# A transformer block on one core: the rows of the attention stacks reordered, and the first batch's loads and sends rearranged

## The chip, the cores and the metric

The kernel runs on one core of a Trainium2 chip. A core has TensorE (matrix products), VectorE (DVE), ScalarE (ACT), GpSimd (POOL), and SyncE (SP), which here only sends DMA transfers. The metric is the device time of one execution in microseconds; lower is better.

## The reference

Four batches of 512 tokens with 128 channels go through one pre-norm block, in float32:

```python
x = x + attn(layernorm(x))     # 16 heads of 8 channels, causal, position slopes on the keys
x = x + ffn(layernorm(x))      # 8 experts, all are summed, times a gate of the token

# attn
scores = q @ k.T / sqrt(8) + slope[head] * key_position      # -inf above the diagonal
y = softmax(scores) @ v ; return y @ w_proj + b_proj
# ffn
logits = rms_normalised(x @ gate_w.T + gate_b) * rms_w ; g = max(softmax(logits / 0.5))
h = gelu(einsum('nd,edh->neh', x, w1) + b1) ; y = einsum('neh,ehd->ned', h, w2) + b2
return (y * g / (g + 1e-6)).sum(axis=1)
```

## The kernel before

**Heads in stacks.** The 16 heads are worked on in 4 sets (s) of 4 heads (q). A head has only 8 channels, so one product serves all rows of the array: `q_stack[i]` holds, for each set, 128 rows by 512 tokens, and `k_stack` holds, for each set and head of it, 128 rows by 512 tokens. To keep float32 precision each value is split into a high and a low part, and a score is the sum of three terms: q_hi with k_hi, q_hi with k_lo, and q_lo with k_hi. Before the change the rows are ordered by term, head and channel: term g of the three fills rows 32 g to 32 g + 31. Rows 96 to 127 hold the position slopes (two rows a head) and, from row 104, the maximum of each query's scores as a high and a low row. The product over 128 rows then gives the finished score; rows of k_stack that belong to other heads are zero.

**How the stacks are filled.** Projection products write q and k of a batch to PSUM; VectorE adds the bias (`take_q`, `take_k`) into `q_full` and `k_full`, ScalarE makes the high parts (`split_high`), GpSimd the low ones (`split_low`). Then DMA transfers inside the core copy them into the stacks. `load_q` sends three transfers of 256 KB: source all 128 rows of q_hi or q_lo, destination 32 rows of the stack. `load_k` (high, SyncE) and `load_k_low` (low, GpSimd) send transfers of 32 KB, for one term, head and half (two sets), each with 8 rows as destination, through `send_k`. `load_max` sends the negated maxima of one set as two transfers of 8 KB. q_stack has two buffers, k_stack one, which is refilled by halves.

**A set's work.** For each set TensorE first computes the scores with zero maxima (`max_unit`, line 720) into the ring `v_ring`; VectorE takes each row's maximum (line 1047). The maxima are transposed, negated (`take_max`) and sent to the stack. Then TensorE computes the scores again, transposed, with the maxima in (`exp_unit`, line 742, and the causal mask, line 748), ScalarE takes the exponential (line 553), and `pv` (line 767) multiplies with v. Beside this, the later stages of the batch before (normalisation, gate, the feed-forward products of lines 673 to 675 and 835) are spread over the 16 places of each set.

**What sets the order.** Every engine runs its own list in program order and waits on semaphores. The places of each unit are written out in tables (`EARLY_PLAN`, `LATER_PLAN`, `STAGES`), which the change leaves alone. The first maximum unit of a batch waits for all three q transfers (`q_loaded`) and for the k transfers of its head. Each DMA-sending engine sends its transfers in the order of its list; SyncE and ScalarE would use two hardware queues, but before the change ScalarE sends nothing.

**The first batch.** It has nothing ahead of it to hide behind. SyncE loads x, w_attn, the constants (580 KB: identity, causal mask, key constants, query constants), the biases and w1. GpSimd clears zeros, makes two small masks, clears rows 0 to 95 of k_stack in two halves (`k_zeros`), and splits w_attn. ScalarE writes the constant rows 96 to 127 of both stacks (`q_constants`, `k_constants`), then makes q_hi and k_hi. TensorE transposes the normalised x, projects q, k and v, and begins the maximum units.

Of the kernel before, what the change touches and what calls it, by code (L numbers as in the profile page):

```python
# [50 lines left out]
CONST_ROWS = 96  # L51
ALIBI_ROWS, MAX_ROWS = 96, 104
# [45 lines left out]
def block_kernel(nc, x, w_attn, w_proj, w1, w2, columns, rows, consts, out):  # L98
# [20 lines left out]
    with ExitStack() as ctx:  # L119
# [103 lines left out]
        cst_loaded = sem("cst_loaded")  # L223
        wa_loaded = sem("wa_loaded")
# [17 lines left out]
        k_zeros = sem("k_zeros")  # L242
# [104 lines left out]
        def _(sp):  # L347
# [10 lines left out]
            def load_q(b):  # L358

                if b >= 2:  # L360
                    sp.wait_ge(e_filled, UNITS * SETS * (b - 1))
                    sp.dma_start(q_stack[b % 2][MAX_ROWS:MAX_ROWS + 2 * QUADS, :, :].bitcast(F32),
                                 zeros[0:2 * QUADS * SETS, :]).then_inc(q_loaded, 16)
                for g, part in ((0, 0), (1, 0), (2, 1)):
                    sp.wait_ge(q_split, 2 * b + part + 1)
                    sp.dma_start(q_stack[b % 2][QR * g:QR * (g + 1), :, :].bitcast(F32),
                                 (q_hi, q_lo)[part][:].bitcast(F32)).then_inc(q_loaded, 16)

            def load_k(b, half):


                if b == 0:
                    sp.wait_ge(k_zeros, half + 1)
                else:

                    sp.wait_ge(e_filled, UNITS * (SETS * (b - 1) + 2 * half + 2))
                sp.wait_ge(k_split, 2 * b + 1)
                for q in range(QUADS):
                    for g in (0, 2):
                        send_k(sp, k_hi, half, g, q, k_loaded[half][q])  # L380

            def load_max(b, s):
                sp.wait_ge(m_ready, SETS * b + s + 1)
                for r, part in ((MAX_ROWS, m_hi), (MAX_ROWS + QUADS, m_lo)):
                    sp.dma_start(q_stack[b % 2][r:r + QUADS, s, :].bitcast(F32),
                                 part[:].bitcast(F32)).then_inc(m_loaded, 16)
# [39 lines left out]
        def _(pool):  # L426
# [22 lines left out]
            def load_k_low(b, half):  # L449

                if b == 0:
                    pool.wait_ge(k_zeros, half + 1)
# [34 lines left out]
            pool.wait_ge(zeros_set, 1)  # L487
            pool.affine_select(out=ident_bf[:], in_=zeros[:, 0:P], compare_op=ALU.not_equal, fill=1.0, base=0,
# [3 lines left out]
            pool.memset(k_stack[0:CONST_ROWS, 0:2, :, :].bitcast(F32), 0.0).then_inc(k_zeros, 1)  # L492
            pool.wait_ge(wa_loaded, 16)
            split(w_attn_sb[:], w_attn_hi[:], w_attn_lo[:], wa_split, 0)
            settle(pool.memset(v_ones[0][:], 0.0))
# [42 lines left out]
        def _(act):  # L538
# [57 lines left out]
            def q_constants(i):  # L596
                for s in range(SETS):
                    act.activation(q_stack[i][CONST_ROWS:P, s, :], zeros[CONST_ROWS:P, :], ACT.Identity,
                                   bias=cst[CONST_ROWS:P, C_QUERY + s:C_QUERY + s + 1]).then_inc(q_const, 1)

            def k_constants(half):
                for q in range(QUADS):
                    act.activation(k_stack[CONST_ROWS:P, 2 * half:2 * half + 2, q, :],  # L603
                                   cst[CONST_ROWS:P, C_KEY:C_KEY + T].unsqueeze(1).to_broadcast([QR, 2, T]),
                                   ACT.Copy, scale=cst[CONST_ROWS:P, C_QUAD + q:C_QUAD + q + 1]).then_inc(k_const, 1)
# [44 lines left out]
        def _(pe):  # L650
# [27 lines left out]
            def transpose_x(b):  # L678
                pe.wait_ge(xn_ready, b + 1)
                if b == 0:  # L680
                    pe.wait_ge(cst_loaded, 16)
# [196 lines left out]
            transpose_x(0)  # L878
            project_qk(0, 0)
            project_qk(0, 1)  # L880
# [52 lines left out]
        def _(dve):  # L933
# [80 lines left out]

            def take_k(b):
                bank_ = v_bank()
                if b >= 1:
# [166 lines left out]
            take_xT(0)  # L1184
            take_q(0)
            take_k(0)
            take_v(0)
            dve.wait_ge(cst_loaded, 16)
# [28 lines left out]
def constants(H, T):  # L1217

    import numpy as np

    SETS = H // QUADS
    c = np.zeros((P, C_QUAD + QUADS), np.float32)
    c[:, C_IDENT:C_IDENT + P] = np.eye(P)
    c[:, C_MASK + T - P:C_MASK + T] = np.where(np.arange(P)[None, :] > np.arange(P)[:, None], MASKED, 0.0)
    slopes = (2.0 ** (-(8.0 / H) * np.arange(1, H + 1))).astype(np.float32)
    high = (slopes.view(np.uint32) & np.uint32(0xFFFFF000)).view(np.float32)
    c[ALIBI_ROWS:MAX_ROWS, C_KEY:C_KEY + T] = np.arange(T)
    c[MAX_ROWS:MAX_ROWS + 2 * QUADS, C_KEY:C_KEY + T] = 1.0
    for q in range(QUADS):
        heads = slice(QUADS * q, QUADS * q + SETS)  # L1230
        c[ALIBI_ROWS + q, C_QUERY:C_QUERY + SETS] = high[heads]
        c[ALIBI_ROWS + QUADS + q, C_QUERY:C_QUERY + SETS] = (slopes - high)[heads]
        c[CONST_ROWS + q:P:QUADS, C_QUAD + q] = 1.0
    return c


def qk_order(a):
# [5 lines left out]
    q = q.reshape(-1, QUADS, 4, 8).swapaxes(-1, -2)  # L1243
# [34 lines left out]
```

## Time and profile before

| what | us |
|---|---|
| median of 3 runs (lowest, highest) | 338.78 (338.53, 339.36) |
| profiled execution, its own time | 340.44 |
| span of its profile | 338.6 |
| TensorE products busy | 298.2 (88%) |
| ScalarE busy | 194.1 (57%) |
| VectorE busy | 190.0 (56%) |
| GpSimd busy | 84.5 (25%) |
| hardware DMA queue | 11.90 MB, 16.2% of 16 engines |

The span is counted from the profile's first instruction. Times at the start of a row are microseconds from there. "SPq" marks SyncE's sends; their time is that of sending, not of the transfer. Short names after an L are lines of the kernel above. Most of the busy time is TensorE's; the question is where it stands still, and for what. PEclk, the clock granted to TensorE, is given as a share of 2.4 GHz: 1.00 is 2.4 GHz and 0.50 is 1.2 GHz.

### The profile page before, as it was taken

To read this page: it belongs to the slowest core of one execution; us is meant where nothing else is said; L and a number is where in the kernel's file an instruction comes from. 1 tells how busy PE (TensorE), PEld (TensorE's weight loads), DVE (VectorE), ACT (ScalarE), POOL (GpSimd) and SP (SyncE) were. 2 spreads that over 40 slices of the span, in tenths; PEclk is the share of its full clock that TensorE was granted. 3 is DMA by queue.
4 is the path that set the end of the run, shared out by engine and by line. 5 is a ranking of instruction groups with operands and counts; after the bars stand their busy time and mean duration, and the time that the engine had idled before them with its cause. 6 is when DMAs were issued, how large, how long until landed. Compare 5 with 4: busy or idle time off the path is not lost.

```text
span 338.6 us, 5507 instructions
## 1 busy us (share of the span) xinstructions
PE 298.2 (88%) x1784; PEld 195.5 (58%) x1784; DVE 190.0 (56%) x787; ACT 194.1 (57%) x322; POOL 84.5 (25%) x213
## 2 busy tenths in 40 slices
PE   0617899969979999699999996999999999998993
PEld 0515565646556676465757664656766665655661
DVE  4417579756786868164777775364877741261011
ACT  1980245544455658386758376567667788534462
POOL 8699012510233046002033153002200320000030
PEclk9999999996999999799999999799999999999999
DMA  6295300170120006101300037002100100000101
GB/s 181 85 131 150 101 4 0 38 110 0 37 76 4 0 17 115 23 2 29 84 2 3 0 82 104 0 2 48 33 4 2 33 2 2 0 2 0 31 1 31
DMA packets 12380, 13.29 MB, mean 39 GB/s; under 512 B 2048, under 2 KB 9088, under 8 KB 12096
## 3 DMA queue, kind: packets, MB, share of 16 engines
q1 hardware_dynamic: 11328, 11.90, 16.2%
q0 software_dynamic: 1024, 1.05, 1.6%
q8 instruction: 14, 0.23, 0.3%
q14 instruction: 14, 0.11, 0.1%
HBM read 5.21 MB, written 1.05 MB: 18 GB/s over the span
## 4 chain that ended last, share of the span: by engine, by line
PE 73%; DVE 9%; DMA 8%; ACT 4%; issue 3%; SPq 1%; POOL 1%; DVEq 0%; ACTq 0%; POOLq 0%
PE ffn_bank L835 16%; PE v_ring L720 11%; PE a_ring L742 11%; PE pv_bank L767 10%; PE a_ring L673 5%; PE a_ring L675 4%; PE a_ring L674 4%; PE a_ring L748 4%; DVE unused L1047 4%; DMA q_stack<-q_lo 4%; DMA k_stack<-k_lo 2%; DMA cst<-consts 2%; PE v_ring L796 1%; ACT k_stack L603 1%; PE v_ring L729 1%
## 5 line engine op out<-in xcount | busy, mean ns | idle before, releaser
L1047 DVE CUSTOM_DVE_ANT_0 unused<-v_ring,cst 128x512 bf16<-128x512 f32 (+3 forms) x256 | 112.5, 488 | 68.1 <-PE v_ring L720 63.5
L553 ACT ACTIVATE probs<-a_ring 128x512 f32<-128x512 f32 (+1 forms) x192 | 92.8, 526 | 77.1 <-PE a_ring L748 76.0
L720 PE MATMUL v_ring<-k_stack,q_stack 128*128 128x512 f32 (+3 forms) x256 | 90.5, 426 | 18.5 <-DMA k_stack<-k_lo 8.4
L742 PE MATMUL a_ring<-q_stack,k_stack 128*128 128x512 f32 (+3 forms) x256 | 77.7, 364 | 0.4 <-DMA q_stack<-m_lo 0.4
L720 PEld LDWEIGHTS v_ring<-k_stack,q_stack 128*128 128x128 f32 x256 | 50.2, 213 | 39.2 <-issue 21.7
L835 PE MATMUL ffn_bank<-hidden,w_sb 128*128 128x512 f32 x128 | 66.3, 602 | 1.1 <-ACT ffn_T L579 0.8
L570 ACT ACTIVATE hidden<-a_ring,cols_sb 128x512 f32<-128x512 f32 x64 | 43.5, 688 | 41.0 <-PE a_ring L675 40.6
L742 PEld LDWEIGHTS a_ring<-q_stack,k_stack 128*128 128x128 f32 x256 | 47.3, 199 | 7.9 <-issue 4.0
L748 PE MATMUL a_ring<-score_mask,ident_bf 128*128 128x128 bf16 (+1 forms) x192 | 48.5, 254 | 0.0
L767 PE MATMUL pv_bank<-probs,v_ones 128*32 128x256 f32 (+3 forms) x512 | 43.2, 447 | 0.0
L324 POOL DMA_DIRECT2D k_stack<-k_lo x32 | 18.3, 573 | 66.1 <-PE a_ring L748 65.3
L673 PE MATMUL a_ring<-zT_hi,w_hi 128*128 128x512 f32 x64 | 33.9, 529 | 0.8 <-DVEq L953 0.8
L748 PEld LDWEIGHTS a_ring<-score_mask,ident_bf 128*128 128x128 bf16 x192 | 18.9, 99 | 21.1 <-issue 14.1
L675 PE MATMUL a_ring<-zT_hi,w_lo 128*128 128x512 f32 x64 | 26.1, 408 | 0.0
L674 PE MATMUL a_ring<-zT_lo,w_hi 128*128 128x512 f32 x64 | 26.1, 408 | 0.0
L835 PEld LDWEIGHTS ffn_bank<-hidden,w_sb 128*128 128x128 f32 x128 | 21.5, 192 | 5.9 <-ACT hidden L570 3.1
L1047 DVE DVE_READ_ACCUMULATOR2_ANT row_max<- 128x1 f32 x256 | 21.4, 83 | 0.0
L673 PEld LDWEIGHTS a_ring<-zT_hi,w_hi 128*128 128x128 f32 x64 | 12.7, 199 | 11.9 <-issue 7.5
L767 PEld LDWEIGHTS pv_bank<-probs,v_ones 128*32 128x32 f32 x512 | 12.4, 110 | 10.0 <-issue 7.0
L330 POOL TENSOR_SCALAR var<-mean_square 128x4 f32<-128x4 f32 x4 | 0.8, 189 | 69.3 <-DVE mean_square L1113 69.2
L570 ACT ACT_TABLE_LOAD x13 | 16.7, 1283 | 0.2
L674 PEld LDWEIGHTS a_ring<-zT_lo,w_hi 128*128 128x128 f32 x64 | 12.6, 197 | 5.1 <-issue 3.6
(109 smaller groups left out, 297.7 us busy)
## 6 DMA issues: line engine op xcount, KB each, us to landing
q_stack<-q_hi SPq DMA_DIRECT2D x8, 256.0 KB
k_stack<-k_hi SPq DMA_DIRECT2D x64, 32.0 KB
x_in<-x SPq DMA_DIRECT2D x4, 256.0 KB, 3.6
hidden<-w SPq DMA_DIRECT2D x1, 1024.0 KB, 8.7
q_stack<-q_lo SPq DMA_DIRECT2D x4, 256.0 KB
k_stack<-k_lo POOLq DMA_DIRECT2D x32, 32.0 KB, 2.5
w_sb<-w SPq DMA_DIRECT2D x1, 1024.0 KB, 5.1
x_res<-x SPq DMA_DIRECT2D x4, 256.0 KB, 3.2
```

The lines of the kernel that those rows point to most:

```text
L324: queue.dma_start(k_stack[QR * g + q * D:QR * g + (q + 1) * D, 2 * half:2 * half + 2, q, :].bitcast(F32), part[rows:rows + QR // 2, :].bit ...
L553: act.activation(probs[:, n % 2, q, KIND_AT[kind]:KIND_AT[kind] + cols], a_bank()[:, 0:cols], ACT.Exp).then_inc(e_freed, 1)
L570: act.activation(hidden[:, n % HB, :], a_bank()[:], ACT.Gelu, bias=b1_cols[:, m:m + 1]).then_inc(g_freed, 1)
L673: pe.matmul(dst, lhs[0], rhs[0], start=True, stop=False)
L674: pe.matmul(dst, lhs[0], rhs[1], start=False, stop=False)
L675: return pe.matmul(dst, lhs[1], rhs[0], start=False, stop=True)
L720: last = pe.matmul(dst[:, at:at + P * (n + 1)], q_stack[b % 2][:, s, n * P:(n + 1) * P], k_stack[:, s, q, 0:P * (n + 1)], start=True, stop ...
L742: pe.matmul(dst[:, at:at + P * (TB - j)], k_stack[:, s, q, j * P:(j + 1) * P], q_stack[b % 2][:, s, j * P:T], start=(at == 0), stop=False, ...
L748: pe.matmul(diagonal, ident_bf[:], score_mask[:].unsqueeze(1).to_broadcast([P, blocks, P]), start=False, stop=True, skip_group_check=True) ...
L767: last = pe.matmul(pv_bank[QR * q:QR * (q + 1), j * P:T], v_ones[b % 2][:, j, s, q, :], probs[:, n % 2, q, at:at + cols], start=(s % 2 == ...
L835: pe.matmul(ffn_bank[:], w2_sb[:, m, :], hidden[:, n % HB, :], start=(m == 0), stop=(m == NT - 1)).then_inc(ffn2_done, 1)
L1047: ins = dve.tensor_tensor_reduce(unused[:, (uses[0] - 1) % V_BANKS, at:at + cols], bank_[:, at:at + cols], cst[:, C_MASK + T - cols:C_MASK ...
```

## The change

**Row order.** The rows of both stacks are ordered by channel, head and term: row 16 d + 4 q + g, for channel d (0 to 7), head q and term g (0 to 2). The fourth row of each head's group of four (g = 3) holds constants: the slopes for d = 4 and 5, the maxima for d = 6 and 7. A transfer of q for one term so writes every fourth row (32 of 128), one of k every sixteenth row from 4 q + g (8 rows), one of the maxima 4 rows at a step of four. The columns of the q projection are permuted on the host to match. The number of transfers, their bytes and their sources are the same, and none of the products changes in size.

**Constants.** With constant rows scattered, `q_constants` and `k_constants` write all 128 rows and so also the zeros; the two fills of k_stack on GpSimd and the semaphore `k_zeros` go, and the q and k transfers of the first use of a buffer wait for `q_const` and `k_const` instead. The constants come in two transfers, keys and queries first, then the mask after w_attn; the identity is made by GpSimd.

**First batch.** ScalarE does one exponential of zeros first, which loads its function table. Keys are projected, taken and split before queries. VectorE makes q_lo in the first batch (`split_q_low`). The first-half key transfers are sent in another order and on two queues: head 0 on SyncE ahead of q, heads 1 and 2 on ScalarE, head 3 on SyncE behind q. The fill of v_ones waits for the normalised x.

SyncE in the first batch, from the load of w1 on, before:

```order
L397 DMA hidden<-w 128x2048
L366 DMA q_stack<-q_hi 32x4x512 [waits q_split] x2
L366 DMA q_stack<-q_lo 32x4x512 [waits q_split]
L324 DMA k_stack<-k_hi 8x2x512 [waits k_split,k_zeros]
L324 DMA k_stack<-k_hi 8x2x512 x7
L324 DMA k_stack<-k_hi 8x2x512 [waits k_split,k_zeros]
L324 DMA k_stack<-k_hi 8x2x512 x7
L401 DMA w_proj_sb<-w_proj 128x128
L402 DMA w_sb<-w 128x2048
```

and now:

```order
L402 DMA hidden<-w 128x2048
L326 DMA k_stack<-k_hi 8x2x512 [waits k_split,k_const]
L326 DMA k_stack<-k_hi 8x2x512
L370 DMA q_stack<-q_hi 32x4x512 [waits q_split,q_const]
L370 DMA q_stack<-q_hi 32x4x512 [waits q_split]
L370 DMA q_stack<-q_lo 32x4x512 [waits q_split]
L326 DMA k_stack<-k_hi 8x2x512 [waits k_split,k_const]
L326 DMA k_stack<-k_hi 8x2x512
L326 DMA k_stack<-k_hi 8x2x512 [waits k_split,k_const]
L326 DMA k_stack<-k_hi 8x2x512 x7
L407 DMA w_proj_sb<-w_proj 128x128
L408 DMA w_sb<-w 128x2048
```

Two key transfers stand ahead of the three of q, two behind them, and the eight of the second half wait for ScalarE's second set of key constants. The row steps don't show in these lines.

ScalarE in the first batch, from its first instruction to its first exponentials of scores, before:

```order
L598 ACT_TABLE_LOAD [waits cst_loaded]
L598 ACTIVATE q_stack<-zeros,cst 32x512 [waits zeros_set]
L598 ACTIVATE q_stack<-zeros,cst 32x512 x3
L603 ACTIVATE k_stack<-cst 32x2x512 x4
L594 ACTIVATE q_hi<-q_full 128x512 [waits q_ready]
L594 ACTIVATE k_hi<-k_full 128x512 [waits k_ready]
L603 ACTIVATE k_stack<-cst 32x2x512 x4
L598 ACTIVATE q_stack<-zeros,cst 32x512 x4
L553 ACTIVATE probs<-a_ring 128x512 [waits e_filled] x8
```

and now:

```order
L614 ACT_TABLE_LOAD
L614 ACTIVATE lge<-zeros 128x32 [waits zeros_set]
L609 ACTIVATE k_stack<-cst 128x2x512 [waits cst_loaded]
L609 ACTIVATE k_stack<-cst 128x2x512 x3
L604 ACTIVATE q_stack<-zeros,cst 128x512 x4
L600 ACTIVATE k_hi<-k_full 128x512 [waits k_ready]
L600 ACTIVATE q_hi<-q_full 128x512 [waits q_ready]
L326 DMA k_stack<-k_hi 8x2x512 [waits k_split,k_const]
L326 DMA k_stack<-k_hi 8x2x512 x3
L609 ACTIVATE k_stack<-cst 128x2x512 x4
L604 ACTIVATE q_stack<-zeros,cst 128x512 x4
L559 ACTIVATE probs<-a_ring 128x512 [waits e_filled] x8
```

The table load no longer stands behind the wait for the constants, the key half comes first, and four sends stand between the split and the second set of constants.

The diff, cut to its core:

```diff
-CONST_ROWS = 96
-ALIBI_ROWS, MAX_ROWS = 96, 104
+ROW_D, ROW_Q, CONST_TERM = 16, 4, 3
+ALIBI_D, MAX_D = 4, 6
+MAX_ROWS = MAX_D * ROW_D + CONST_TERM
...
         def send_k(queue, part, half, g, q, loaded):
             rows = QR * q + half * QR // 2
-            queue.dma_start(k_stack[QR * g + q * D:QR * g + (q + 1) * D, 2 * half:2 * half + 2, q, :].bitcast(F32),
+            queue.dma_start(k_stack[ROW_Q * q + g::ROW_D, 2 * half:2 * half + 2, q, :].bitcast(F32),
                             part[rows:rows + QR // 2, :].bitcast(F32)).then_inc(loaded, 16)
...
+                if b < 2:
+                    sp.wait_ge(q_const, SETS * (b + 1))
                 for g, part in ((0, 0), (1, 0), (2, 1)):
                     sp.wait_ge(q_split, 2 * b + part + 1)
-                    sp.dma_start(q_stack[b % 2][QR * g:QR * (g + 1), :, :].bitcast(F32),
+                    sp.dma_start(q_stack[b % 2][g::ROW_Q, :, :].bitcast(F32),
                                  (q_hi, q_lo)[part][:].bitcast(F32)).then_inc(q_loaded, 16)
...
-            def load_k(b, half):
+            def load_k(b, half, quads=range(QUADS)):
                 if b == 0:
-                    sp.wait_ge(k_zeros, half + 1)
+                    sp.wait_ge(k_const, QUADS * (half + 1))
...
             load_x(0)
+            sp.dma_start(cst[:, C_KEY:], consts[:, C_KEY:]).then_inc(cst_loaded, 16)
             sp.dma_start(w_attn_sb[:], w_attn).then_inc(wa_loaded, 16)
-            sp.dma_start(cst[:], consts).then_inc(cst_loaded, 16)
+            sp.dma_start(cst[:, C_MASK:C_KEY], consts[:, C_MASK:C_KEY]).then_inc(mask_loaded, 16)
...
+            load_k(0, 0, [0])
             load_q(0)
-            load_k(0, 0)
+            load_k(0, 0, [3])
             load_k(0, 1)
...
-            pool.memset(k_stack[0:CONST_ROWS, 0:2, :, :].bitcast(F32), 0.0).then_inc(k_zeros, 1)
...
-            pool.memset(k_stack[0:CONST_ROWS, 2:4, :, :].bitcast(F32), 0.0).then_inc(k_zeros, 1)
-            split_low(0, 1)
             split_low(0, 0)
...
             act.wait_ge(zeros_set, 1)
+            act.activation(lge[:], zeros[:, 0:TB * E].rearrange("p (n e) -> p n e", n=TB), ACT.Exp)
             act.wait_ge(cst_loaded, 16)
+            k_constants(0)
             q_constants(0)
-            k_constants(0)
+            split_high(0, 0)
             split_high(0, 1)
-            split_high(0, 0)
+            act.wait_ge(k_const, QUADS)
+            act.wait_ge(k_split, 1)
+            for q in (1, 2):
+                for g in (0, 2):
+                    send_k(act, k_hi, 0, g, q, k_loaded[0][q])
             k_constants(1)
             q_constants(1)
...
             transpose_x(0)
+            project_qk(0, 1)
             project_qk(0, 0)
-            project_qk(0, 1)
...
+            def split_q_low():
+                dve.wait_ge(q_split, 1)
+                dve.tensor_tensor(q_lo[:], q_full[:], q_hi[:].bitcast(F32), ALU.subtract).then_inc(q_split, 1)
...
+            take_k(0)
             take_q(0)
-            take_k(0)
+            split_q_low()
             take_v(0)
...
-    q = q.reshape(-1, QUADS, 4, 8).swapaxes(-1, -2)
+    q = q.reshape(-1, QUADS, 4, 8).transpose(0, 3, 1, 2)
```

## Rows read from the trace of the kernel before

**Rows 1.** The page, busy microseconds and share of the span of each engine.

```profile
PE 298.2 (88%) x1784; PEld 195.5 (58%) x1784; DVE 190.0 (56%) x787; ACT 194.1 (57%) x322; POOL 84.5 (25%) x213
```

**Rows 2.** Waits, whole span: who waits for what, total us, times, longest.

```profile
PE v_ring L720 <- DMA k_stack<-k_lo: 8.4, 1, 8.4
```

**Rows 3.** Timeline of TensorE: start, us, instruction, in brackets the idle time before.

```profile
76.06 1.19 PE L720 MATMUL v_ring<-k_stack,q_stack 128*128 128x512 f32 x3 [2.72 <-issue]
...
79.44 0.73 PE L742 MATMUL a_ring<-q_stack,k_stack 128*128 128x512 f32 x1
...
138.65 0.74 PE L720 MATMUL v_ring<-k_stack,q_stack 128*128 128x512 f32 x3 [2.66 <-DMA q_stack<-q_lo]
...
211.73 1.10 PE L720 MATMUL v_ring<-k_stack,q_stack 128*128 128x512 f32 x3 [2.70 <-DMA q_stack<-q_lo]
```

**Rows 4.** Stretches: length, busy (instructions) of PE, PEld, DVE, ACT, POOL; clock, DMA, GB/s.

```profile
76.00:82.00 6.00, 5.94 (x23) 3.82 (x24) 3.64 (x16) 1.31 (x3) 0.00 (x0) 0.50 0.00 0
140.00:144.00 4.00, 4.00 (x11) 3.16 (x12) 0.58 (x4) 1.53 (x3) 0.00 (x0) 0.57 0.00 0
211.00:217.00 6.00, 5.27 (x22) 3.57 (x23) 1.39 (x6) 1.53 (x3) 0.00 (x0) 0.72 0.00 0
```

**Rows 5.** Timeline of SyncE at the later batches: start, us of sending.

```profile
68.00 1.25 SPq L366 DMA_DIRECT2D q_stack<-q_hi  x2
69.29 0.61 SPq L366 DMA_DIRECT2D q_stack<-q_lo  x1
...
72.80 0.68 SPq L385 DMA_DIRECT2D q_stack<-m_lo  x1
...
131.70 0.61 SPq L366 DMA_DIRECT2D q_stack<-q_lo  x1
...
204.35 0.60 SPq L366 DMA_DIRECT2D q_stack<-q_lo  x1
```

**Rows 6.** Stretches with q transfers and with the w2 load, columns as above.

```profile
18.00:24.00 6.00, 0.00 (x0) 0.00 (x0) 0.88 (x4) 5.84 (x8) 5.25 (x10) 1.00 1.10 130
132.00:136.00 4.00, 3.99 (x42) 2.16 (x40) 2.97 (x12) 2.98 (x8) 1.74 (x3) 1.00 1.08 141
32.00:36.00 4.00, 2.85 (x9) 2.01 (x8) 3.15 (x13) 0.00 (x0) 1.24 (x3) 1.00 0.98 359
```

**Rows 7.** DMA issues: times, KB each, median us from issue to landing.

```profile
x_in<-x SPq DMA_DIRECT2D x4, 256.0 KB, 3.6
...
out<-result SPq DMA_DIRECT2D x4, 256.0 KB, 2.2
...
cols_sb<-columns SPq DMA_DIRECT2D x1, 17.0 KB, 4.9
```

**Rows 8.** Timelines of VectorE, ScalarE, SyncE and TensorE in the first batch.

```profile
14.28 0.75 DVE L1011 TENSOR_SCALAR q_full<-v_ring,cols_sb 128x512 f32<-128x512 f32 x1 [1.90 <-PE v_ring L675]
15.33 0.63 ACT L594 ACTIVATE q_hi<-q_full 128x512 fp32r<-128x512 f32 x1
16.50 0.63 ACT L594 ACTIVATE k_hi<-k_full 128x512 fp32r<-128x512 f32 x1 [0.54 <-DVEq L1021]
17.16 4.25 ACT L603 ACTIVATE k_stack<-cst 32x1024 fp32r<-32x1024 f32 x4
...
17.37 0.61 SPq L366 DMA_DIRECT2D q_stack<-q_lo  x1
18.10 11.60 SPq L324 DMA_DIRECT2D k_stack<-k_hi  x16
...
26.33 1.08 PE L720 MATMUL v_ring<-k_stack,q_stack 128*128 128x512 f32 x2 [8.36 <-DMA k_stack<-k_lo]
...
30.22 0.54 SPq L402 DMA_DIRECT2D w_sb<-w  x1
...
35.99 0.64 SPq L385 DMA_DIRECT2D q_stack<-m_lo  x1
...
38.05 0.76 PE L742 MATMUL a_ring<-q_stack,k_stack 128*128 128x512 f32 x1 [0.42 <-DMA q_stack<-m_lo]
```

More of the change, by code:

```diff
@@ L223, in block_kernel @@
         cst_loaded = sem("cst_loaded")
+        mask_loaded = sem("mask_loaded")
+        ident_set = sem("ident_set")
         wa_loaded = sem("wa_loaded")
@@ L241, in block_kernel @@
         q_const = sem("q_const")
-        k_zeros = sem("k_zeros")
         k_const = sem("k_const")
@@ L377, in load_k @@
                 sp.wait_ge(k_split, 2 * b + 1)
-                for q in range(QUADS):
+                for q in quads:
                     for g in (0, 2):
@@ L383, in load_max @@
                 sp.wait_ge(m_ready, SETS * b + s + 1)
-                for r, part in ((MAX_ROWS, m_hi), (MAX_ROWS + QUADS, m_lo)):
-                    sp.dma_start(q_stack[b % 2][r:r + QUADS, s, :].bitcast(F32),
+                for r, part in ((MAX_ROWS, m_hi), (MAX_ROWS + ROW_D, m_lo)):
+                    sp.dma_start(q_stack[b % 2][r:r + ROW_D - CONST_TERM:ROW_Q, s, :].bitcast(F32),
                                  part[:].bitcast(F32)).then_inc(m_loaded, 16)
@@ L451, in load_k_low @@
                 if b == 0:
-                    pool.wait_ge(k_zeros, half + 1)
+                    pool.wait_ge(k_const, QUADS * (half + 1))
                 else:
@@ L487, in _ @@
             pool.wait_ge(zeros_set, 1)
+            pool.affine_select(out=ident, in_=zeros[:, 0:P], compare_op=ALU.not_equal, fill=1.0, base=0,
+                               pattern=[[1, P]], channel_multiplier=-1).then_inc(ident_set, 1)
             pool.affine_select(out=ident_bf[:], in_=zeros[:, 0:P], compare_op=ALU.not_equal, fill=1.0, base=0,
@@ L597, in q_constants @@
                 for s in range(SETS):
-                    act.activation(q_stack[i][CONST_ROWS:P, s, :], zeros[CONST_ROWS:P, :], ACT.Identity,
-                                   bias=cst[CONST_ROWS:P, C_QUERY + s:C_QUERY + s + 1]).then_inc(q_const, 1)
+                    act.activation(q_stack[i][:, s, :], zeros[:], ACT.Identity,
+                                   bias=cst[:, C_QUERY + s:C_QUERY + s + 1]).then_inc(q_const, 1)
             def k_constants(half):
                 for q in range(QUADS):
-                    act.activation(k_stack[CONST_ROWS:P, 2 * half:2 * half + 2, q, :],
-                                   cst[CONST_ROWS:P, C_KEY:C_KEY + T].unsqueeze(1).to_broadcast([QR, 2, T]),
-                                   ACT.Copy, scale=cst[CONST_ROWS:P, C_QUAD + q:C_QUAD + q + 1]).then_inc(k_const, 1)
+                    act.activation(k_stack[:, 2 * half:2 * half + 2, q, :],
+                                   cst[:, C_KEY:C_KEY + T].unsqueeze(1).to_broadcast([P, 2, T]),
+                                   ACT.Copy, scale=cst[:, C_QUAD + q:C_QUAD + q + 1]).then_inc(k_const, 1)
             act.wait_ge(zeros_set, 1)
+            act.activation(lge[:], zeros[:, 0:TB * E].rearrange("p (n e) -> p n e", n=TB), ACT.Exp)
             act.wait_ge(cst_loaded, 16)
+            k_constants(0)
             q_constants(0)
-            k_constants(0)
+            split_high(0, 0)
             split_high(0, 1)
-            split_high(0, 0)
+            act.wait_ge(k_const, QUADS)
[3 more added lines that the diff above has]
+                    send_k(act, k_hi, 0, g, q, k_loaded[0][q])
             k_constants(1)
@@ L680, in transpose_x @@
                 if b == 0:
-                    pe.wait_ge(cst_loaded, 16)
+                    pe.wait_ge(ident_set, 1)
                 dst = v_bank()
@@ L1013, in take_q @@
                 dve.sem_inc(q_ready, 1)
+            def split_q_low():
+                dve.wait_ge(q_split, 1)
+                dve.tensor_tensor(q_lo[:], q_full[:], q_hi[:].bitcast(F32), ALU.subtract).then_inc(q_split, 1)
             def take_k(b):
                 bank_ = v_bank()
-                if b >= 1:
+                if b == 0:
+                    dve.wait_ge(rows_loaded, 32)
+                else:
                     dve.wait_ge(k_split, 2 * b)
@@ L1184, in _ @@
             take_xT(0)
+            take_k(0)
             take_q(0)
-            take_k(0)
+            split_q_low()
             take_v(0)
-            dve.wait_ge(cst_loaded, 16)
+            dve.wait_ge(mask_loaded, 16)
             for k in range(UNITS):
@@ L1226, in constants @@
     high = (slopes.view(np.uint32) & np.uint32(0xFFFFF000)).view(np.float32)
-    c[ALIBI_ROWS:MAX_ROWS, C_KEY:C_KEY + T] = np.arange(T)
-    c[MAX_ROWS:MAX_ROWS + 2 * QUADS, C_KEY:C_KEY + T] = 1.0
     for q in range(QUADS):
         heads = slice(QUADS * q, QUADS * q + SETS)
-        c[ALIBI_ROWS + q, C_QUERY:C_QUERY + SETS] = high[heads]
-        c[ALIBI_ROWS + QUADS + q, C_QUERY:C_QUERY + SETS] = (slopes - high)[heads]
-        c[CONST_ROWS + q:P:QUADS, C_QUAD + q] = 1.0
+        alibi = [ROW_D * d + ROW_Q * q + CONST_TERM for d in range(ALIBI_D, MAX_D)]
+        maxima = [ROW_D * d + ROW_Q * q + CONST_TERM for d in range(MAX_D, 8)]
+        c[alibi, C_KEY:C_KEY + T] = np.arange(T)
+        c[maxima, C_KEY:C_KEY + T] = 1.0
+        c[alibi[0], C_QUERY:C_QUERY + SETS] = high[heads]
+        c[alibi[1], C_QUERY:C_QUERY + SETS] = (slopes - high)[heads]
+        c[alibi + maxima, C_QUAD + q] = 1.0
     return c
```

3 lines of the change are left out of this document (2 added, 1 removed).

## The prediction, made before the change was run

> **What bounds the kernel now.** I read the page first. TensorE is busy 88% of the span [rows 1], so most of the time is its own work, and a change that removes no TensorE work can only win where TensorE stands still. The list of waits says where that is: TensorE's longest wait for a transfer is 8.4 us, once, for data of the first batch [rows 2]. Its own timeline shows three more stops, one ahead of each later batch, that name a transfer into q_stack or "issue": 2.72 us before 76.06 (the one put down to "issue"), 2.66 us before 138.65 and 2.70 us before 211.73, always at the first product of the new batch's q_stack [rows 3]. Together 8.08 us. The granted clock then shows a second price: after each stop TensorE runs for a while at 1.2 instead of 2.4 GHz. The mean granted share is 0.50 over 76 to 82, 0.57 over 140 to 144 and 0.72 over 211 to 217 [rows 4].
>
> Why these stops? SyncE sends the batch's q_stack as three transfers of 256 KB, the first at 68.00 and the last at 69.29 [rows 5], and the product at 76.06 is the first to need all three. The DMA engines are all busy then, but move only 141 GB/s (132 to 136), and 130 GB/s in the same work of the first batch (18 to 24). The weights loaded at 32 to 36 move at 359 GB/s with the same 16 engines [rows 6]. So 768 KB at 130 GB/s take 5.9 us, and TensorE, which is ready 5.3 us after the first send (76.06 less 2.72 is 73.34, less 68.00), waits for the rest and the landing.
>
> **The row layout, in every batch.** Each of the three transfers writes 32 rows of q_stack. Before, they are 32 neighbours; after, every fourth row of the whole 128. Bytes, sends, and the source (all 128 rows of q_hi or q_lo) stay. No row shows such a destination, so its rate is bounded from both sides: no gain, 130 GB/s, and the 359 GB/s of a load that writes all 128 rows. I take a value near the upper one: the source is no limit, as the result is read from 128 rows and 256 KB of it lands 2.2 us after its issue, x_in, written to 128 rows, in 3.6 us [rows 7]; what is peculiar to the slow transfer is the narrow destination. To close the stop the last q transfer must land 5.3 us after the first send. With about 1.9 us for sending and landing (m_lo, 8 KB, is sent at 35.99 and used at 38.05 [rows 8]) 3.4 us are left for 768 KB: 226 GB/s. With 2.2 to 3.6 us from its own send, the last transfer of the second boundary (sent 131.70) lands at 133.9 to 135.3, and TensorE is ready at 135.99; in the third 204.35 becomes 206.6 to 208.0 against 209.03.
>
> The Trainium skill has a rule for it. "SBUF — State Buffer", section "Door 1: The DMA port swizzle", gives the memory 16 DMA ports, of which 32 adjacent partitions reach 8 (189 GB/s at 1 MiB) and 128 reach 16 (328). Rows at a step of four reach all 16 by its map. An estimate from that page: 130 times 328/189 is 226 GB/s, which just closes the stop. No row here shows the ports themselves; that the slow transfers are those to adjacent rows agrees.
>
> So the three stops go: 8.1 us. With them goes the slow clock. What it costs is the missing share of each window: 0.50 of 6 us, 0.43 of 4 us and 0.28 of 6 us [rows 4], 3.0, 1.7 and 1.7 us. In the first VectorE is a partner in the pace (3.64 of 6 us busy), so I count 2.4 there: 5.8 us together. Elsewhere it counts in full: TensorE has no gap in 140 to 144. What is late next at these places is the maxima's pair of sends: m_lo is sent at 72.80 [rows 5] and takes 2.06 us to be used, 74.9, while TensorE wants it 3.4 us after 76.06 (79.44 [rows 3]) at half the clock, so from about 2 us after 73.34 at the full one, an estimate. That is close, and VectorE, which rested during the stops, will be asked earlier: I take off 0.4 us per boundary, 1.2 us. The boundaries give 8.1 + 5.8 - 1.2 = 12.7 us, and between zero and 14.5 us at the bounds.
>
> The k rows (8 per transfer) move from 8 neighbours to every sixteenth row. Beyond the first batch no wait names them; nothing is counted.
>
> **The first batch.** The keys come first now. ScalarE's k_hi takes the place of q_hi at 15.33, which follows the constants without a gap; VectorE had written its data by 15.03 (14.28 plus 0.75). So all that lets ScalarE be free earlier (constants in parts, the table load ahead of them, no fills of k_stack on GpSimd) is worth 0 to 0.3 us; I take 0, as a hand-over costs something. The constants now write 128 rows instead of 32, with as many elements in a row, and keep their length. q_hi takes the place of k_hi at 16.50 and ends at 17.13 [rows 8]. SyncE then sends: two k transfers from 15.95 (0.72 us each) to 17.4, two of q_hi to 18.7, q_lo from 18.7. Before, q_lo was sent at 17.37: 1.3 us later now. VectorE makes q_lo in the meantime, hidden ahead of v. With the wider destination it lands 2.2 to 3.6 us after, at 20.9 to 22.3. The first product, at 26.33 now, then starts at about 22.3: 4.0 us earlier.
>
> But that is not what the batch gains. SyncE's later sends are set by the second half of the constants. ScalarE now does four sends itself (0.6 to 0.7 us each, 17.1 to 20.0), and then the 4.25 us of k constants: 24.2. Only then may SyncE send eight k transfers, 5.7 us, to 29.9. That is where w_proj is sent now (18.10 plus 11.60). So w2, x_res and x_in, 1,536 KB, are sent from 30.22 on, three sends of about half a microsecond, to 31.8 as now [rows 8], and drain at 359 GB/s until about 36.3 [rows 6]. The second send of the maxima starts 9.7 us after the first product (35.99 less 26.33), which would be 32.0, but SyncE is free for the two only from 31.8, so they leave at 31.8 and 32.5, behind these 1,536 KB on the same queue. What a small transfer behind a large one does is shown by cols_sb: 17 KB sent right after the 580 KB of constants land 4.9 us after issue, later than x_in's 256 KB with 3.6 [rows 7]. So the maxima land at 36.4 to 36.9, and the first score product starts at about 36.8 instead of 38.05 [rows 8]: 1.2 us. The cover for the other 2.3 us is this queue. TensorE and VectorE do the early maxima of the next set meanwhile, as now. The second half's sends, the GpSimd work behind its own wait for the same constants (v_ones, the w1 split, some 2 to 3 us later than now) and q_stack's constants for batch 1 all end before 40, long before they are asked for: nothing.
>
> **Sum.** 12.7 + 1.2 = 13.9 us. The profiled execution took 340.44 us with a span of 338.6; after, 326.5 with a span of 324.7. The median of the timed runs lies 1.66 us below that execution, so **324.9 us**, 4.1% less.
>
> **Rivals.**
> A, the maxima are not held: their few rows slip past the loads. For it: they are only 8 KB each. Against: cols_sb. The first score product then starts at 32.5 + 2.06 = 34.6, 3.5 us earlier: 322.6 us.
>
> B, the wide destination gives only part, about 180 GB/s, because three transfers in a row still meet at the same rows. 768 KB take 4.3 us, 1.6 less, and stops of 1.1 us stay. 4.8 us of the stops; with the clock it is 332.8 if it still falls, 329.9 if it falls half as much. Taken as 331. For it: no row shows a transfer inside the core above 141 GB/s over several microseconds. Against: the store and the wide loads.
>
> C, the layout does nothing, since the limit is such a copy itself: only the first batch's 1.2 us at the most, 337.6.
>
> D, slower. As C, and in the first batch the three q transfers stand 1.3 us later in SyncE's queue, behind the keys, at the old rate. The first product starts at 27.7, m_lo is sent at 37.3, past the drain of w2, and all that follows shifts by 1.3 us: 340.1. It decides while the rate stays at or under about 135 GB/s; at 168 the shorter load (4.6 us) already makes up for the later send, and each boundary gains besides. For it: the k transfers run at the same time on all queues. Against: the rate of the wide loads.
>
> **Chances.** Forecast 0.66 (its own range 321.5 to 328), A 0.10, B 0.13, C 0.06, D 0.05. This kernel's runs can tell about 0.3% (1 us) from no change. A and B and the forecast are faster, C is split between faster and the same: faster 0.91, same 0.04, slower 0.05. The range reaches down past A, to 320.5 (all of the boundaries' 14 us and 3.5 at the start give 321.3), and up through B to 332.5.
>
> **What would show it.** In the profile after: no wait of TensorE on q_stack<-q_lo above 0.5 us at the three boundaries; a granted clock of 1.00 throughout from about 40 us on; the DMA rate during the q transfers above 220 GB/s; k transfers of the second half sent by SyncE from about 24; the first product of q_stack near 22.3 and the first score product near 36.8 with a wait of 2 us or more on m_lo before it. The forecast is wrong if the q transfers still move at 130 to 140 GB/s (C, D), or if each stop is replaced by one of similar length on the maxima, or if the clock falls at other places.

## The result, and the profile after

| | us |
|---|---|
| before, median of 4 runs beside it (lowest, highest) | 338.65 (336.1, 339.36) |
| after, median of 4 runs (lowest, highest) | 324.15 (323.41, 324.44) |
| ratio, 95% interval | 0.958 (0.953 to 0.963) |
| predicted | 324.9 (320.5 to 332.5) |
| span of the profile, before and after | 338.6, 322.4 |

The change makes the kernel 4.2% faster, 0.7 us more than forecast. The page of the profile after has TensorE busy 6.4 us less than [rows 1], though it does the same 1784 products, and the clock's line, which had a 6 and two 7s among its 40 slices before, holds 9 throughout (its first 42 us are taken up further down):

```profile
PE 291.8 (91%) x1784; PEld 191.4 (59%) x1784; DVE 190.1 (59%) x788; ACT 193.9 (60%) x323; POOL 76.1 (24%) x211
...
PEclk9999999999999999999999999999999999999999
```

TensorE's timeline at the three boundaries answers [rows 3]. Each row is start, length, instruction; an idle time would stand in brackets, and there is none:

```profile
69.72 1.07 PE L779 MATMUL pv_bank<-probs,v_ones 128*32 128x384 f32 x16
70.72 0.73 PE L732 MATMUL v_ring<-k_stack,q_stack 128*128 128x512 f32 x3
...
128.26 0.50 PE L732 MATMUL v_ring<-k_stack,q_stack 128*128 128x512 f32 x1
...
196.97 0.50 PE L732 MATMUL v_ring<-k_stack,q_stack 128*128 128x512 f32 x1
```

What made it so is the rate of the q transfers. They move at 356 GB/s where they moved at 130 to 141 [rows 6]. The columns are those of [rows 4]: at the end the clock, the share of the DMA engines and GB/s. In the stretches of [rows 4] TensorE now has the full clock; they are other work of the same kernel, since all is earlier:

```profile
66.00:68.00 2.00, 2.00 (x20) 1.37 (x19) 1.98 (x10) 1.87 (x5) 0.49 (x1) 1.00 0.96 356
76.00:82.00 6.00, 6.00 (x57) 3.45 (x56) 4.08 (x19) 3.29 (x9) 2.12 (x4) 1.00 0.07 16
140.00:144.00 4.00, 4.00 (x25) 1.92 (x23) 2.51 (x13) 2.07 (x5) 0.00 (x0) 1.00 0.00 0
211.00:217.00 6.00, 6.00 (x52) 3.71 (x45) 2.73 (x13) 3.33 (x6) 2.26 (x4) 1.00 0.15 32
```

The first batch, to be read against [rows 8]. These are rows of the timelines of ScalarE, SyncE and TensorE:

```profile
14.94 0.63 ACT L600 ACTIVATE k_hi<-k_full 128x512 fp32r<-128x512 f32 x1 [3.79 <-DVEq L1040]
16.22 0.63 ACT L600 ACTIVATE q_hi<-q_full 128x512 fp32r<-128x512 f32 x1 [0.65 <-DVEq L1025]
16.29 3.07 ACTq L326 DMA_DIRECT2D k_stack<-k_hi  x4
18.47 0.64 SPq L370 DMA_DIRECT2D q_stack<-q_lo  x1
19.21 9.51 SPq L326 DMA_DIRECT2D k_stack<-k_hi  x10
19.41 4.26 ACT L609 ACTIVATE k_stack<-cst 128x1024 fp32r<-128x1024 f32 x4 [2.56 <-issue]
22.84 1.51 PE L732 MATMUL v_ring<-k_stack,q_stack 128*128 128x512 f32 x4 [5.15 <-DMA q_stack<-q_lo]
29.25 0.43 SPq L408 DMA_DIRECT2D w_sb<-w  x1
32.53 0.65 SPq L389 DMA_DIRECT2D q_stack<-m_lo  x1
36.16 0.77 PE L754 MATMUL a_ring<-q_stack,k_stack 128*128 128x512 f32 x1 [2.02 <-DMA q_stack<-m_lo]
```

The first product is 3.5 us earlier (22.84 against 26.33), the first score product only 1.9 us (36.16 against 38.05), and before it TensorE now waits 2.02 us for the maxima.

One column of these traces has to be read with care: the clock in the first batch. The stretch behind the first score product reads 1.00 in the changed kernel and 0.50 in step_four, an experiment below with the same start:

```profile
36.00:42.00 6.00, 5.84 (x22) 4.19 (x22) 2.28 (x11) 3.13 (x6) 0.00 (x0) 1.00 0.00 0
36.00:42.00 6.00, 5.06 (x17) 3.55 (x18) 2.08 (x9) 2.39 (x4) 0.00 (x0) 0.50 0.02 6
```

Yet the first score products have the same length in both, 0.77 us for one of 512 columns. From 48 us on, where both traces say 1.00, such a product takes 0.40 to 0.47 us in the changed kernel. So the first batch ran at half the clock in the changed kernel too, up to about 41 us, and in the kernel before up to about 45, though their clock lines say 1.00 there. At the three boundaries the column and the lengths agree.

**Where the 16.2 us of the span went** can be read off the send of each set's m_lo, as the same instruction stands in both traces. Before minus after: 2.5 us ahead of the first boundary (72.80 and 70.28), 7.7 behind it (88.05 and 80.39); 7.6 (135.46 and 127.82) and 12.0 (156.66 and 144.69) around the second; 12.0 (208.49 and 196.53) and 16.3 (229.66 and 213.40) around the third. So the boundaries gave 5.1, 4.3 and 4.3 us, 13.8 together, and the first batch 2.5. Less the stops of 2.72, 2.66 and 2.70 us, the clock behind them cost 2.4, 1.7 and 1.6 us. These sizes are those of one execution of the kernel before, a long one (340.44 us); between the medians the gain is 14.5 us and not 16.2.

### The profile page after: what moved, and what is told of

Read it like the earlier page. It is cut to its first block, busy times and chain, and to the rows that moved or that the text cites. A ratio compares the mean times of both kernels' runs of the same rounds, so it can differ in the third digit from the quotient of the medians.

```text
span 322.4 us, 5513 instructions
## 1 busy us (share of the span) xinstructions
PE 291.8 (91%) x1784; PEld 191.4 (59%) x1784; DVE 190.1 (59%) x788; ACT 193.9 (60%) x323; POOL 76.1 (24%) x211
## 4 chain that ended last, share of the span: by engine, by line
PE 81%; DVE 10%; DMA 3%; issue 2%; ACT 1%; SPq 1%; DVEq 0%; ACTq 0%
PE ffn_bank L847 17%; PE a_ring L754 12%; PE v_ring L732 12%; PE pv_bank L779 11%; PE a_ring L685 5%; PE a_ring L760 5%; PE a_ring L687 4%; PE a_ring L686 4%; DVE unused L1066 4%; PE v_ring L808 1%; DMA q_stack<-q_lo 1%; PE v_ring L685 1%; PE v_ring L741 1%; DMA q_stack<-m_lo 1%; PE v_ring L686 1%
## 5 line engine op out<-in xcount | busy, mean ns | idle before, releaser
L732 PE MATMUL v_ring<-k_stack,q_stack 128*128 128x512 f32 (+3 forms) x256 | 88.5, 417 | 7.3 <-DMA q_stack<-q_lo 5.1
L754 PE MATMUL a_ring<-q_stack,k_stack 128*128 128x512 f32 (+3 forms) x256 | 76.6, 359 | 2.0 <-DMA q_stack<-m_lo 2.0
L732 PEld LDWEIGHTS v_ring<-k_stack,q_stack 128*128 128x128 f32 x256 | 48.6, 206 | 27.5 <-issue 17.1
L754 PEld LDWEIGHTS a_ring<-q_stack,k_stack 128*128 128x128 f32 x256 | 46.5, 196 | 9.5 <-issue 5.6
L779 PE MATMUL pv_bank<-probs,v_ones 128*32 128x256 f32 (+3 forms) x512 | 42.3, 440 | 0.0
L685 PE MATMUL a_ring<-zT_hi,w_hi 128*128 128x512 f32 x64 | 33.0, 516 | 0.8 <-DVEq L965 0.8
L760 PEld LDWEIGHTS a_ring<-score_mask,ident_bf 128*128 128x128 bf16 x192 | 18.7, 97 | 20.5 <-issue 13.1
L687 PE MATMUL a_ring<-zT_hi,w_lo 128*128 128x512 f32 x64 | 25.2, 393 | 0.0
L686 PE MATMUL a_ring<-zT_lo,w_hi 128*128 128x512 f32 x64 | 25.1, 393 | 0.0
```

The source lines that it names most:

```text
L685: pe.matmul(dst, lhs[0], rhs[0], start=True, stop=False)
L686: pe.matmul(dst, lhs[0], rhs[1], start=False, stop=False)
L687: return pe.matmul(dst, lhs[1], rhs[0], start=False, stop=True)
L732: last = pe.matmul(dst[:, at:at + P * (n + 1)], q_stack[b % 2][:, s, n * P:(n + 1) * P], k_stack[:, s, q, 0:P * (n + 1)], start=True, stop ...
L754: pe.matmul(dst[:, at:at + P * (TB - j)], k_stack[:, s, q, j * P:(j + 1) * P], q_stack[b % 2][:, s, j * P:T], start=(at == 0), stop=False, ...
L760: pe.matmul(diagonal, ident_bf[:], score_mask[:].unsqueeze(1).to_broadcast([P, blocks, P]), start=False, stop=True, skip_group_check=True) ...
```

## Experiments

Each ran beside runs of the kernel before on the same chip (medians of 338.65 to 339.38 us). The kernel before scatters by some 2%, the kernels near 324 us by about 0.3%; so the intervals of the ratios, half a per cent to each side, don't tell these kernels apart, and their medians come from different chips. A difference of about 1 us between two of them is therefore read from the traces too, most simply from the m_lo sent ahead of the first boundary: at 70.28 in the changed kernel.

### rows_only

Only the row order; the first batch's order is as before.

```diff
-            load_k(0, 0, [0])
             load_q(0)
-            load_k(0, 0, [3])
+            load_k(0, 0)
...
-            k_constants(0)
             q_constants(0)
-            split_high(0, 0)
+            k_constants(0)
             split_high(0, 1)
-            act.wait_ge(k_const, QUADS)
-            act.wait_ge(k_split, 1)
-            for q in (1, 2):
-                for g in (0, 2):
-                    send_k(act, k_hi, 0, g, q, k_loaded[0][q])
+            split_high(0, 0)
...
```

Projections, takes, constant loads and the table load are put back likewise.

> The changed kernel's row order, with loads, key and query order, sends and tables of the first batch put back as before (the two fills of k_stack stay away, and the second half's key sends still wait for the constants). Theory (the row order makes the q transfers wide, and that is nearly all of the gain; at the start the drain of w2 sets the first score product in any case): no stops at the three boundaries, clock at 1.00 from 45 us on, first product of q_stack at 22 to 23, first score product at 36.2 to 37, time 324.5 to 325.5 us. Rival (the rearranged first batch is worth some us by itself): first score product at 38, time 326.5 to 328 us.

Measured: 325.22 us, ratio 0.956 (0.951 to 0.961). The row order alone has all of the boundary gain, and no wait of TensorE on a q transfer is left after the first batch. In the first batch:

```profile
22.54 1.51 PE L722 MATMUL v_ring<-k_stack,q_stack 128*128 128x512 f32 x4 [3.43 <-ACT k_stack L605]
...
36.82 0.77 PE L744 MATMUL a_ring<-q_stack,k_stack 128*128 128x512 f32 x1 [2.98 <-DMA q_stack<-m_lo]
```

The first product starts even earlier than in the full change; the first score product comes 0.66 us later, after a longer wait for the maxima. Here w2 is sent at 29.98, 0.73 us later than 29.25. That is the order of what the rest of the change is worth: m_lo ahead of the first boundary is sent 0.9 us later (71.22), and the medians differ by 1.1 us; the ratios, 0.956 here and 0.958 for the change, don't show it. From there to the first m_lo behind the boundary both take 10.1 us, where the kernel before took 15.3.

### start_only

The counterpart: the whole rearranged first batch, with the old row order.

```diff
-            queue.dma_start(k_stack[ROW_Q * q + g::ROW_D, ...
+            queue.dma_start(k_stack[BASE[g] + STEP * D * q:BASE[g] + STEP * (D * (q + 1) - 1) + 1:STEP, ...
-                    sp.dma_start(q_stack[b % 2][g::ROW_Q, :, :].bitcast(F32),
+                    sp.dma_start(q_stack[b % 2][BASE[g]:BASE[g] + STEP * 31 + 1:STEP, :, :].bitcast(F32),
...
```

BASE is (0, 32, 64, 96) and STEP is 1; maxima, slopes and the host's permutation follow.

> The changed kernel with the rows of both stacks in the old order (32 neighbours for a term); all of the rearranged first batch stays. Theory: q transfers at 130 to 140 GB/s, stops of 2.6 to 2.8 us at the three boundaries and the half clock behind them as before, first product at 26 to 27.7, time 337.5 to 340 us (rivals C and D of the prediction). Rival (part of the boundary gain comes from the new order of sends or from the constants): stops shorter than 2 us, time under 334 us.

Measured: 341.29 us, ratio 1.007 (1.003 to 1.011): slower than before by 0.7%, and above the 337.5 to 340 us expected. The stops are back:

```profile
PE v_ring L732 <- DMA q_stack<-q_lo: 15.3, 3, 10.1
PE v_ring L732 <- issue: 2.8, 1, 2.8
```

and the first batch loses 1.5 us, at the old rate of 130 GB/s over 18 to 24:

```profile
27.84 1.51 PE L732 MATMUL v_ring<-k_stack,q_stack 128*128 128x512 f32 x4 [10.06 <-DMA q_stack<-q_lo]
...
39.54 0.77 PE L754 MATMUL a_ring<-q_stack,k_stack 128*128 128x512 f32 x1 [0.40 <-DMA q_stack<-m_lo]
```

This is rival D of the prediction, with its place (27.7 was given) and about its size (340.1). Keys ahead of queries are a loss if the q transfers stay slow.

The half clock came back behind two of the stops only. Behind the third, of 2.70 us as in the kernel before, the clock stayed whole:

```profile
212.85 0.73 PE L732 MATMUL v_ring<-k_stack,q_stack 128*128 128x512 f32 x3 [2.70 <-DMA q_stack<-q_lo]
...
213.00:217.00 4.00, 4.00 (x24) 2.89 (x25) 1.39 (x6) 1.91 (x3) 0.00 (x0) 1.00 0.00 0
```

Read by the same sends of m_lo against the changed kernel, the three boundaries cost 5.9, 4.1 and 2.8 us in this execution, 12.8 together instead of 13.8. So a stop of this length doesn't always bring the half clock; what decides isn't shown.

### step_two

Is it enough that the rows are not neighbours? Here a q transfer writes every second row of one half of the memory's 128 rows, so 32 rows are spread over 63.

```diff
-ROW_D, ROW_Q, CONST_TERM = 16, 4, 3
+BASE, STEP = (0, 1, 64, 65), 2
...
```

All else is as in start_only.

> The changed kernel with another row order: a q transfer writes every second row of one half of the memory (rows 0, 2 .. 62, or 1, 3 .. 63, or 64, 66 .. 126), a key transfer 8 rows at a step of two. Rival one, any destination that isn't neighbours is fast: no stops, 324 to 326 us. Theory, the port map of the Trainium skill's page SBUF — State Buffer (by it 64 rows of one half reach no more ports than 32 neighbours): the q transfers stay near 130 to 180 GB/s, stops of 1 to 2.7 us at the boundaries, 331 to 339 us. Between them, if the rate rises in proportion to the rows' spread: 180 to 200 GB/s.

Measured: 337.96 us, ratio 0.995 (0.991 to 0.998). The stops are nearly whole. TensorE's timeline at the three boundaries, and the stretches with q transfers in the first, second and third batch:

```profile
74.33 0.71 PE L732 MATMUL v_ring<-k_stack,q_stack 128*128 128x512 f32 x3 [2.73 <-issue]
...
135.93 0.73 PE L732 MATMUL v_ring<-k_stack,q_stack 128*128 128x512 f32 x3 [2.64 <-DMA q_stack<-q_lo]
...
208.56 0.87 PE L732 MATMUL v_ring<-k_stack,q_stack 128*128 128x512 f32 x3 [2.27 <-DMA q_stack<-q_lo]
```

```profile
18.00:24.00 6.00, 0.00 (x0) 0.00 (x0) 0.55 (x3) 4.32 (x5) 2.04 (x4) 1.00 0.99 162
67.50:71.50 4.00, 4.00 (x43) 2.27 (x41) 2.66 (x13) 2.45 (x7) 0.00 (x0) 1.00 1.07 160
129.50:133.50 4.00, 3.79 (x41) 2.00 (x39) 2.77 (x12) 3.03 (x7) 1.58 (x3) 1.00 1.10 136
```

With all DMA engines busy (shares of 0.99 to 1.10) the transfers move at 136 to 162 GB/s. So a gap between the rows isn't enough. In the first batch the small rise does count: the first product starts at 25.33, 2.5 us before that of start_only (27.84). By the port map of the Trainium skill's page "SBUF — State Buffer", section "Door 1: The DMA port swizzle", 64 rows of one half reach the same eight ports as 32 neighbours, and rows at a step of four over all 128 reach sixteen; both rates go with that. The ports themselves show in no trace.

### step_four

Which part of the order matters? Here q's destination is the very one of the change (every fourth row), while a key transfer writes 8 rows at a step of 4 within 32 rows, instead of at a step of 16 over the whole. The edit is shown against step_two.

```diff
-BASE, STEP = (0, 1, 64, 65), 2
+BASE, STEP = (0, 1, 2, 3), 4
```

> The changed kernel with the terms interleaved at a step of four but head and channel in the old order: a q transfer writes the same every fourth row as now, a key transfer 8 rows at a step of 4 inside one quarter of the memory (32 rows) instead of at a step of 16. Theory (the gain is in q's destination): no stops, 323.5 to 325 us, as the changed kernel. Rival (the keys' spread matters too, as their sends became shorter, 0.63 us instead of 0.71): key sends at 0.7 us again, the first batch some tenths of a us later, 325 to 326.5 us.

Measured: 325.07 us, ratio 0.956 (0.952 to 0.961). The boundaries are free, so q's destination is what counts. The keys' spread is worth about 1 us, in the first batch, by way of SyncE: the m_lo ahead of the first boundary is sent 1.0 us later (71.29), and the medians differ by 0.9 us (the ratios, 0.956 and 0.958, don't show it). A group of eight key sends takes 5.69 us here, and 5.07 in the changed kernel:

```profile
60.75 5.69 SPq L326 DMA_DIRECT2D k_stack<-k_hi  x8
```

In the first batch w2 is therefore sent at 30.09 instead of 29.25, and the first score product starts at 36.94 instead of 36.16.

### before_fill

The kernel before, with TensorE kept at work through its stops.

```diff
+            def fill(dst):
+                for _ in range(FILL):
+                    pe.matmul(dst[:, 0:512], w_attn_hi[:, 0:P], w1_hi[:, 0:512], start=True, stop=True)
...
+                if b >= 1 and s == 0 and k == 0:
+                    fill(dst)
+                    pe.wait_ge(q_loaded, q_count(b + 1))
...
```

FILL is 11. The unit's wait for its bank stands ahead of the fill, its waits for q and keys behind it.

> The kernel before, with 11 products of 512 columns whose result is overwritten put ahead of the wait for q_stack at the start of batches 1 to 3, so that TensorE works through the 2.7 us in which it would stand still. The stops of 8.1 us remain as time. Theory (idleness at the stops brings the half clock, and it costs 5.8 us): the clock stays at 1.00 behind the boundaries, time 332.5 to 334 us. Rival (the half clock is covered by VectorE and ScalarE): the clock stays up and the time is 337.5 to 339 us. If the clock falls all the same: 338.7 us and the idleness is not its cause.

Measured: 335.04 us, ratio 0.984 (0.978 to 0.990). The stops stay as time, filled with products that nobody uses:

```profile
73.36 2.79 PE L709 MATMUL v_ring<-w_hi,w_attn_hi 128*128 128x512 f32 x11
76.15 0.74 PE L731 MATMUL v_ring<-k_stack,q_stack 128*128 128x512 f32 x3
```

and the clock behind them is whole. The same stretch had 0.50 in [rows 4]:

```profile
76.00:82.00 6.00, 5.87 (x40) 3.90 (x39) 5.22 (x25) 2.78 (x6) 0.00 (x0) 1.00 0.01 3
```

The other two stretches of [rows 4] read 1.00 here as well. The span falls from 338.6 to 333.4, by 5.2 us, and the medians by 4.2. So idleness at the stops did bring the half clock in the kernel before, and it cost 4 to 5.5 us beside the 8.1 us of the stops. The estimate had been 5.8.

The median is 1.0 us above the expected range. The fill overshoots the stops by 0.1 us each, and the first score product starts 0.3 us later (38.34) for a reason that isn't shown. The larger part is a matter of bookkeeping: the price of 5.8 us was read from the profiled execution of the kernel before, which took 340.44 us, and taken off the median, 338.78. The two profiled executions, 340.44 and 335.17 us, differ by 5.3.

### weights_early

What holds the first maxima? Here w_proj, w2 and x_res are sent right behind w1.

```diff
             sp.dma_start(w1_sb[:], w1).then_inc(w1_loaded, 16)
+            sp.dma_start(w_proj_sb[:], w_proj).then_inc(wp_loaded, 16)
+            sp.dma_start(w2_sb[:], w2).then_inc(w2_loaded, 16)
+            load_residual(0)
...
```

The three are taken out behind load_k(0, 1).

> The changed kernel with w_proj, w2 and x_res sent right behind w1, in the first batch's idle stretch of the DMA engines (12 to 17 us), so that of the 1,536 KB ahead of the first maxima only x_in's 256 KB stay. Theory (the drain of these loads holds the first maxima back by 1.6 us): m_lo is used 2.1 us after its send instead of 3.6, the first score product starts at 34.6 instead of 36.16, time 322.4 to 323 us. Rival (a set's maxima take this time whatever is ahead of them, or VectorE's early maxima bind instead): 36 us, 324 us. If the earlier w2 delays q's transfers: first product after 23.5 and up to 1 us lost.

Measured: 322.60 us, ratio 0.950 (0.945 to 0.955). m_lo is sent at 32.46, as in the changed kernel (32.53), but used 1.9 instead of 3.6 us later:

```profile
34.36 0.77 PE L754 MATMUL a_ring<-q_stack,k_stack 128*128 128x512 f32 x1 [0.27 <-DMA q_stack<-m_lo]
```

The queue was the hold. The m_lo ahead of the first boundary is sent 1.9 us earlier (68.42), and the median is 1.5 us under that of the changed kernel.

### maxima_first

The same from the other side: the two sends stand ahead of the loads in SyncE's list.

```diff
             load_k(0, 1)
+            load_max(0, 0)
             sp.dma_start(w_proj_sb[:], w_proj).then_inc(wp_loaded, 16)
...
```

The old call behind load_x(1) is taken out.

> The changed kernel with the first maxima's two sends ahead of w_proj, w2, x_res and x_in in SyncE's list. Theory: m_hi is sent at 31.7, m_lo at 32.3, used at 34.4, time 322.4 to 323.2 us; the loads go out at 33 to 35 and are in time for the next batch's x (asked for at 45) and for w2. Rival (the loads are then late for x of batch 1 or the queue isn't the hold): 324 us or more.

Measured: 322.12 us, ratio 0.949 (0.944 to 0.953), the fastest kernel of the study. It is not told apart from weights_early by the intervals. The first score product starts at 34.33, and no wait of TensorE on a transfer remains behind it, so the loads are in time.

```profile
34.33 0.77 PE L754 MATMUL a_ring<-q_stack,k_stack 128*128 128x512 f32 x1 [0.28 <-DMA q_stack<-m_lo]
```

The first score product is 1.8 us earlier than in the changed kernel, the m_lo ahead of the first boundary only 1.2 (69.04): TensorE's products here take 7.2 us from the first score product to reach the length of the full clock, and 5.3 in the trace of the changed kernel.

### one_queue

Do the key sends on ScalarE's queue pay?

```diff
-            load_k(0, 0, [3])
+            load_k(0, 0, [1, 2, 3])
...
-            act.wait_ge(k_const, QUADS)
-            act.wait_ge(k_split, 1)
-            for q in (1, 2):
-                for g in (0, 2):
-                    send_k(act, k_hi, 0, g, q, k_loaded[0][q])
```

> The changed kernel with the four key sends of ScalarE given back to SyncE (heads 1 to 3 behind q). Theory (the second queue pays nothing: ScalarE's four sends push its second set of key constants back by some 2.6 us, and SyncE waits for these): ScalarE's constants start at 16.9 instead of 19.4, SyncE sends without a pause, w_proj at 28.5 to 29.2 as now (28.76), first product at 22.8, time 323.8 to 324.6 us. Rival (the second queue saves SyncE four sends): w_proj 2.5 us later, first score product at 38 or later, time 326 to 327 us.

Measured: 323.71 us, ratio 0.955 (0.952 to 0.959); the changed kernel had 324.15. In the traces almost nothing is between them: both spans are 322.4 us, and the m_lo ahead of the first boundary is sent at 70.27 and 70.28. SyncE does all sixteen sends and is done no later (w_proj at 28.43, 28.76 with two queues), since ScalarE's constants come earlier:

```profile
16.63 4.25 ACT L609 ACTIVATE k_stack<-cst 128x1024 fp32r<-128x1024 f32 x4
...
19.04 9.35 SPq L326 DMA_DIRECT2D k_stack<-k_hi  x14
```

The second queue gains nothing here. ScalarE pays 3.07 us of sending ahead of the very constants for which SyncE's next sends wait.

## Why the prediction was right, point by point

- **The q transfers get wide.** Right, and the value taken near the upper bound was the true one: 356 GB/s, against 359 for the wide load and 226 needed. Rivals B and C fell. step_two shows that a spread over one half isn't enough; nothing between one half and the whole was run.
- **The stops go, 8.1 us.** Right: no idle time is left at any of the three places.
- **The slow clock goes, 5.8 us.** Right in kind, and before_fill shows it apart from the stops. 8.1 and 5.8 make 13.9; the boundaries gave 13.8, with 2.4, 1.7 and 1.6 us for the clock where 2.4, 1.7 and 1.7 were counted. That is so close because both are read from the same execution of the kernel before; start_only's had 12.8 for the three.
- **The deduction of 1.2 us for what is late next** was the mis-sized term of the boundaries: nothing was late. In the first one the maxima, sent at 70.28, are used at 73.03 without a wait. The boundaries were put at 12.7 and gave 13.8 us.
- **First product at 22.3.** It came at 22.84. q_lo was sent at 18.47 (18.7 was said) but landed 4.2 us after its send, not 2.2 to 3.6: the transfers of keys and of q share the engines there, which the sum had left out. The same microsecond, 19 to 20, in rows_only, where q goes ahead of the keys, and in the changed kernel:

```profile
19.00:20.00 1.00, 0.11 (x1) 0.00 (x0) 0.85 (x4) 1.00 (x2) 0.62 (x1) 1.00 1.02 379
19.00:20.00 1.00, 0.00 (x0) 0.00 (x0) 0.00 (x0) 0.59 (x1) 0.97 (x2) 1.00 1.02 244
```

- **It is not what the batch gains, as the maxima wait behind w2.** Right, and shown by weights_early and maxima_first. The size was off by 0.6 us: 36.16 for 36.8. SyncE was free of its key sends at 28.7 and not at 29.9, as such a send takes 0.63 instead of 0.71 us with the new rows, and ScalarE's constants began at 19.4 (its sends started while q_hi was still being made). The prediction had the keys' new rows at nothing; step_four puts them at about 1 us. This is the term that it had left out.
- **1.2 us for the first batch** was too little: 2.5. Of that 1.9 stand at the first score product. The other 0.6 come just behind it: TensorE's products reach the length of the full clock at 41.5, 5.3 us after the first score product, where before it took until 45, 7 us. That it came up sooner need not be the change's doing: in maxima_first, with the same start, it took 7.2 us again. What sets it isn't shown.
- **ScalarE free earlier is worth 0 to 0.3 us**, taken as 0. Right in kind: ScalarE now idles for 3.79 us ahead of k_hi, so it isn't what holds it. But k_hi starts at 14.94 where q_hi had started at 15.33, 0.39 us earlier: VectorE itself begins to write k_full at 14.00, where it had begun with q_full at 14.28, and the bound had taken that as fixed.
- **Two queues.** The step said that ScalarE's sends push its constants back, and gave the second queue no term; one_queue agrees.

The sum had two errors of the same sign, 1.1 and 1.3 us, which make 2.4 us of span; the span fell by 16.2 instead of 13.9. Against the medians only 0.7 us of that shows, and this is luck: the prediction took 1.66 us off for the distance between the profiled execution and the median, which was right before (340.44 and 338.78) and is nothing after (324.16 and 324.15). An error of 1.7 us of the other sign so hid most of the two.

## What to carry to other kernels

When a transfer keeps all DMA engines busy at a third of the rate of a plain load, look at which rows it writes, not at its bytes: 32 neighbouring rows, or 32 rows spread over one half, moved at 130 to 162 GB/s, and 32 rows spread evenly over all 128 at 356. A stop of TensorE can have a second price in the clock behind it, here half as much again or more over three stops, and nothing behind one stop of the same length in start_only; so read the granted clock after each idle time before you size a wait. And a small transfer on the critical path doesn't belong behind a megabyte on the same queue: moving one call in one list gave another 2 us between the medians, 1.2 us between the profiles.

## What the runs showed of the hardware that was not expected

- The row step of a destination changes even the time of sending. SyncE takes 5.07 us for eight key sends at a step of 16 rows, and 5.69 at a step of 4 (step_four), 2 (step_two) or 1 (the kernel before).
- Spreading the rows within one half (step_two) raises the rate a little, unevenly: 160 and 162 GB/s in two stretches, 136 in the third.
- Stops of the same length don't always bring the half clock: 2.70 us did in the kernel before (0.72 over 211 to 217) and didn't in start_only (1.00 over 213 to 217).
- The clock that a trace shows for its first 45 us or so can be wrong: 1.00 in one trace and 0.50 in another over products of the same length. There the lengths of equal products tell more.
